# Attention: the products of probabilities and values of two head groups one behind the other in every second quad

## The reference, cut to what matters

```python
qkv = x @ w_qkv + b_qkv                      # x: (8, 256, 256), 16 heads of 16 features
q, k, v = split into heads, each (8, 16, 256, 16)
att = einsum('bhqd,bhkd->bhqk', q, k) * scale
att = softmax(where(causal, att, -inf), axis=-1)
y = einsum('bhqk,bhkd->bhqd', att, v)
x = layernorm(x + y.reshape(8, 256, 256) @ w_proj + b_proj)
# then cross attention over ctx (3 rounds with a GRU cell), layernorm,
# then 16 experts of 64, the best 4 of each position, layernorm
```

## Time and profile before

| | |
|---|---|
| median of 3 runs | 669.06 us (667.75 to 669.28) |
| span of the profiled execution | 664.9 us |
| TensorE busy | 621.7 us, 93% |
| VectorE busy | 493.7 us, 74% |
| ScalarE busy | 327.0 us, 49% |
| GpSimd busy | 225.2 us, 34% |
| mean granted clock of TensorE | 0.982 |
| attention stage | about 28 to 211 us of the span |

### The profile page before, as it was taken

How to read it: one execution, slowest core, us unless ns; L and a number is a source line. 1 busy time by engine, 2 the same in 40 slices (tenths; PEclk the granted TensorE clock), 3 DMA queues, 4 the chain that set the end, 5 groups by cost and what they waited for, 6 DMA issues and landing times.

```text
span 664.9 us, 13964 instructions
## 1 busy us (share of the span) xinstructions
PE 621.7 (93%) x5064; PEld 565.3 (85%) x5064; DVE 493.7 (74%) x1039; ACT 327.0 (49%) x734; POOL 225.2 (34%) x274
## 2 busy tenths in 40 slices
PE   5988998998999999999999999999999998899996
PEld 4766787776767989999899998999989988799996
DVE  4755474674764788879888799887999888767653
ACT  5444553553575355655556555565566644231320
POOL 9402332432453251422223232232312213352543
PEclk9799898997999999999999999999999999999999
DMA  8634646357400040010000000000000000042240
GB/s 283 203 103 146 173 135 190 93 173 217 121 18 1 1 160 0 2 33 2 0 0 0 32 0 0 0 0 0 0 1 1 1 1 1 16 147 82 80 157 34
DMA packets 31374, 43.34 MB, mean 65 GB/s; under 512 B 3072, under 2 KB 18912, under 8 KB 31328
## 3 DMA queue, kind: packets, MB, share of 16 engines
q1 hardware_dynamic: 31328, 42.73, 21.1%
HBM read 29.39 MB, written 13.21 MB: 64 GB/s over the span
## 4 chain that ended last, share of the span: by engine, by line
PE 56%; DVE 13%; issue 13%; DMA 5%; SPq 5%; POOL 4%; ACT 3%; DVEq 0%; POOLq 0%; ACTq 0%
PE bank L448 26%; PE bank L2171 11%; PE bank L1991 4%; POOL hid_hl L801 3%; DMA k_rows<-k_hl 3%; PE bank L1891 2%; DMA q_op<-negT 2%; PE bank L1977 1%; PE bank L456 1%; PE bank L1849 1%; PE bank L2008 1%; SPq L519 1%; PE bank L1856 1%; PE bank L1872 1%; PE bank L2000 1%
## 5 line engine op out<-in xcount | busy, mean ns | idle before, releaser
L448 PE MATMUL bank<-slots_hl,whhT_hl 128*128 128x256 f32 x864 | 113.1, 284 | 0.0
L448 PEld LDWEIGHTS bank<-slots_hl,whhT_hl 128*128 128x128 f32 x864 | 105.5, 188 | 2.4 <-ACT gate_z L1104 1.0
L1293 DVE TENSOR_REDUCE neg_max<-bank 128x2 f32<-128x512 f32 (+1 forms) x96 | 65.7, 690 | 55.2 <-PE bank L1858 41.3
L2171 PE MATMUL bank<-attn_hl,vg_hl 128*128 128x256 f32 x864 | 105.7, 280 | 0.1
L2171 PEld LDWEIGHTS bank<-attn_hl,vg_hl 128*128 128x128 f32 x864 | 100.9, 188 | 4.3 <-ACT attn_hl L815 3.9
L870 ACT ACTIVATE pT<-bank 128x512 f32<-128x512 f32 x96 | 56.9, 598 | 57.7 <-PE bank L1872 41.7
L682 POOL TENSOR_SCALAR_AFFINE_SELECT pT<-pT 128x512 f32<-128x512 f32 x64 | 40.6, 638 | 117.5 <-ACT pT L870 117.4
L696 POOL TENSOR_TENSOR sq<-sq 128x256 f32<-128x256 f32 x24 | 18.1, 754 | 170.6 <-ACT sq L1089 130.3
L801 POOL TENSOR_TENSOR hid_hl<-hid,hid_hl 128x512 fp32r<-128x512 f32 x32 | 40.9, 1303 | 25.8 <-ACT hid_hl L815 25.7
L448 PE MATMUL bank<-x2T_hl,keys_hl 128*128 128x256 f32 x384 | 48.6, 284 | 0.0
L448 PE MATMUL bank<-values_hl,hid_hl 128*128 128x256 f32 x384 | 47.8, 281 | 0.3 <-DVE x L1567 0.3
(11 more groups left out here) (212 smaller groups left out, 1298.2 us busy)
## 6 DMA issues: line engine op xcount, KB each, us to landing
gate_rows<-gate_mem SPq DMA_DIRECT2D x48, 128.0 KB, 3.1
q_rows<-q_hl SPq DMA_DIRECT2D x21, 256.0 KB
k_rows<-k_hl SPq DMA_DIRECT2D x21, 256.0 KB
q_op<-q_rows SPq DMA_DIRECT2D x28, 192.0 KB, 3.2
k_op<-k_rows SPq DMA_DIRECT2D x14, 384.0 KB, 4.4
x_in<-in_x_dram SPq DMA_DIRECT2D x8, 256.0 KB, 6.6
c_in<-in_ctx_dram SPq DMA_DIRECT2D x8, 256.0 KB, 4.8
out_dram<-y_out SPq DMA_DIRECT2D x8, 256.0 KB, 2.8
```

The source lines that it names most:

```text
L448: mm = pe.matmul(dst, left(a), right(b), start=first and n == 0, stop=last and n == 2, skip_group_check=True)
L1293: dve.tensor_reduce(dst, src, AX.X, ALU.max, negate=True).then_inc(max_ok, 1)
L2171: mm = pe.matmul(halves(b)[:, m, :], vg_hl[:, j, v_part, 3 * t + r, q:q + P], attn_hl[:, j, at_part, t, :], start=n == 2 and a + m + t == ...
```

## The change

In TensorE's loop the group of heads no longer comes once in each quad. In every even quad from 2 on, behind `turned` of third 1, two groups run one behind the other: that of the quad two back and that of the quad before. Odd quads have none. The instructions, their operands, banks and waits are the same; the work beside keeps its places. The last pair is that of quads 30 and 31, in quad 32.

```diff
                     if 0 <= quad < QUADS:
                         turned(quad, third)
-                    if third == 2 and 0 <= quad - 1 < QUADS:
+                    if third == 1 and quad % 2 == 0 and 0 <= quad - 2 < QUADS:
+                        heads(quad - 2)
                         heads(quad - 1)
                     for name, n in beside(quad, third):
                         work_beside(name, n)
```

## The result

The changed kernel takes 671.14 us against 667.34 us of the kernel before (medians of 6 runs each): 1.0059 times, with a 95% interval of 1.0032 to 1.0086. That is 3.8 us slower, clear of no change. Forecast was +3.2 us. The profiled execution spans 669.5 us against 664.9. Executions that the record marks as slow (three in all) are left out of the ratios and of mean clocks.

A forecast was written before the change was run, and what follows sets the result against it. TensorE decides one half of each eight-quad period, SyncE and its DMAs the other. Terms 1.2 + 0.8 + 1.9 - 0.7 = +3.2 us on 669.06 gave 672.3 us, 8-in-10 range 668.9 to 675.3.

The forecast's parts named there:

- A pair costs 1.59 us: TensorE: one group costs 0.89 us, a second right behind it 0.70, so a pair 1.59 instead of 1.78.
- Quads 4 to 7, +1.2: TensorE: +0.47 us waiting for the bank `y_nat` frees, then +0.70 from the pair at quad 6.
- SyncE's halves, +0.8: Quads 8 and 16: k projection behind the pair makes `k_hl` late for SyncE, +0.05 to 0.1 and +0.75 us.
- Quads 12 to 15, +1.9: Chain from exp of (12, 2) through GpSimd and VectorE to `neg` starts 1.2 us later; quad 14's pair adds 0.70.
- Quad 20 to the end, -0.7: Seven pairs for 13 single groups -0.44 us, `y_nat` waits +0.5 each at quads 22 and 26, tail -1.25.
- The tail's filled idle time: Idle time that ScalarE's exp ended, 0.23 and 1.02 us, is filled by moved work: -1.25 us.
- the wait that I had put before `neg` for `y_nat`: Quad 26: TensorE reaches `neg` 0.89 us sooner and waits for `y_nat`, +0.5 us.
- The waits at quads 4, 12 and 20: TensorE's waits for the maxima's DMA lengthen to about 3 us, 3.1 at quad 12, 3.8 at quad 20.
- The clock: Number of TensorE stretches at 1.2 GHz taken as unchanged; 1.7 us either way kept for the range.
- rival 2: Longer TensorE waits cost one or two more 3.4 us stretches at 0.50: +1.7 to 3.4 us; chance 0.13.
- Rivals 1 and 3: Second group in a pair: rival 1, 0.89 us, 674.8 us, chance 0.12; rival 3, 0.35 us, 667.7 us, chance 0.08.
- rival 4: New waits at `y_nat` and the norm chain smaller, taken up by slack: +0.1 us, 669.2 us; chance 0.17.

The follow-up runs named there:

- e1: Changed kernel with `turned` of third 1 put between the two groups of each pair; 673.67 us, 1.0102 times the kernel before.
- e3: Changed kernel with pairs only at places 4 and 6 (quad % 8), single groups in third 2 elsewhere; 671.2 us, 1.0082 times the kernel before.
- e4: Changed kernel with the second k projection ahead of the pair at place 0 (quad % 8); 671.25 us, 1.005 times the kernel before.
- e6: Changed kernel with the layer norm's power ahead of `text_lo` on GpSimd; 669.16 us, 1.0023 times the kernel before.
- e10: Kernel before with the norm's power ahead of `text_lo` on GpSimd and pairs only in quads 30 and 32; 663.15 us, 0.9956 times the kernel before.

## Why the prediction was right, point by point

The time was forecast at 672.3 us from a median of 669.06, so +3.2; it came +3.8. The mechanism held in the main, and most terms came out near their size. That the total did too has luck in it: the clock, taken as unchanged, was not, and the 669.06 that the forecast starts from is the median of three executions, 2.8 us above the mean of the 75 timed on other occasions (666.2). The changed kernel's mean of 671.3 is 5.1 us above that: near the forecast's 3.2 and 1.8 for the clock. By the terms of the sum, each against the mean of the two profiles of before:

- **A pair costs 1.59 us.** It costs 1.44 + 0.10 = 1.54; the second group 0.65 instead of 0.70. e1 shows the saving. What is paid once less per pair is the edge between strips and the full array. The Trainium skill, TensorEngine Tiling (Array Packing), Key Properties, has it that a change of the tiling mode drains TensorE; by that rule a pair is cheaper than two groups, and the trace agrees, with 1.44 us for 1.58.
- **Quads 4 to 7, +1.2.** 19.2 against 18.2: +1.0. The wait for `y_nat` is there with 0.42 us. e3 has the same 19.2. TensorE's own part, two pairs for three groups, is only 2 x 1.54 - 3 x 0.89 = +0.4 us of it.
- **SyncE's halves, +0.8.** From turned to L497 +0.6 at each of the two: +1.2. The whole columns give +0.9 and +0.5, but e3, with nothing at place 0, has about as much (+0.6 and +1.2), so the columns don't show whose it is. That `k_hl` releases L497 was right, the working of it was not: I took the k projection as what is late and had 0.1 and 0.75 from two single issue times. The low part of k waits behind the next maximum on VectorE (e4), and SyncE's own run to L497 differs by up to 0.8 us from case to case.
- **Quads 12 to 15, +1.9.** 21.7 against 19.8: +1.9, with a wait of 2.46 us for `y_nat`; e6 takes 0.9 of it away by shortening the chain on GpSimd.
- **Quad 20 to the end, -0.7.** 16.7 against 15.8: +0.9. 16.5 against 15.9: +0.6. Tail 21.4 against 23.5: -2.1. Together -0.6. The tail's filled idle time was as forecast. At quad 26 the wait that I had put before `neg` for `y_nat` is one of 0.91 us before `natural` for the maxima: VectorE's norm waits there for GpSimd's power, behind the mask of the quad whose exp the pair delays, the same chain as at quad 14. At quads 10 and 18 it is hidden in SyncE's half.
- **The waits at quads 4, 12 and 20** were forecast at about 3, 3.1 and 3.8 us and came at 1.73, 2.84 and 2.34, and the prediction called itself wrong if they didn't lengthen. Against the profile it was made from (1.78, 2.46, 2.50) only quad 12 did; against the second (1.39, 2.08, 1.81) all three did. They differ that much between executions of one kernel. At quads 12 and 20 the 0.91 us before them eats part of what the missing group leaves.
- **The clock** was taken as unchanged: 24 us at 0.50 in the first profile of before, 17 in the second, 27.5 in that of after, over the whole span. It moved from place to place between executions of one kernel, so single profiles don't settle it. The means of all executions do: 23.4 us for 17.8, a cost of 1.8 us by the estimate and at most 2.8. This term is missing from the sum; it is the size of rival 2's one more stretch. The rule named beside it (the Trainium skill, TensorE: Matmul & The Clock Gate, What's actually happening: activity releases the throttle) is not contradicted by these rows. But that it is the longer waits for the maxima which hold the clock low is not shown: e6 has such waits of 2.55, 2.65 and 3.06 us, and a mean clock of 0.9855.

The sum of the measured terms, 1.0 + 1.2 + 1.9 - 0.6 = 3.5 us, has the clock's share taken off, so it answers to the 5.1 us between the means less 1.8, that is 3.3, rather than to the 3.8 between the medians of six. Behind the `yT` of quad 33 the span is 450.2 us for 449.5 and 452.4, so the later stages did only shift. Rivals 1 and 3, on the second group's price, are excluded by the 1.44 us; rival 4 by the waits before `neg`, the lengths of the halves and the interval of the result. Rival 2 is not excluded: it holds beside the forecast's own terms, with its cause open.

## What to carry to other kernels

Saving a switch between column strips and the full array is real (0.24 us for each pair here), but what decides is on which side of a DMA-bound point the work lands: moved out of a stretch where TensorE waits anyway into one where it doesn't, it costs time, and through the chains of the other engines it can cost more than its own length (+1.0 and +1.9 us here, where TensorE's own work grew by 0.4). Before moving work on one engine, mark where its queue stands for something that doesn't depend on it, and count what falls on each side. And where a wait looks like room to gain, look what arrives next: here the operands' DMAs stood within a microsecond or two of the maxima's. Last, compare the mean granted clock of all executions, not of one profile: halves set right for the clock hid a cost of about 2 us that came by the clock.

## What the runs showed that was not expected

- VectorE's two norm instructions (L1336, both on 128x256) take 0.72 us together at quad 21 of the kernel before, and 1.99 to 2.15 us where GpSimd's L670, an operation with two inputs, runs beside the second of them, at quad 13 of the kernel before, of the changed one and of e10.
- One and the same kernel differs in where its clock is lowered: after the wait of quad 4, 3.4 us at 0.50 in one execution and none in the other, though the waits were 1.78 and 1.39 us.
- SyncE's run of issues from turned(7, 2) or (15, 2) to L497 takes 7.5 to 8.3 us where no pair stands at place 0, so a wait of its queue found in one execution can be hidden in the next.
